# A Mamba round in which DMAs that GpSimd issues add up the softplus, and ScalarE scales a fifth state

## The chip, the cores and the metric

The kernel runs on one core of a Trainium2 chip. The metric is the device time of one execution in microseconds. A core has five engines that are spoken of here: TensorE (PE in the profile, PEld for its weight loads), VectorE (DVE), ScalarE (ACT), GpSimd (POOL) and SyncE (SP), which only issues DMAs. They run side by side and meet only at semaphores. GpSimd can compute and can issue DMAs, one after the other in its own program order.

## The reference

A two-layer model works on `x` of 8 sequences of 512 tokens with 128 features. Layer 0 (attention and a routed feed-forward block) is not touched by the change. Layer 1 is a Mamba block beside a gated feed-forward block:

```python
xv = x @ W_in ; xv = silu(causal_conv(xv, 4 taps) + conv_b)     # 256 channels
ssm = xv @ W_x                                                   # dt_raw (8), B (16), C (16)
delta = softplus(dt_raw @ W_dt + b_dt)
dA  = exp(delta[..., None] * A)                                  # 16 states
dBx = delta[..., None] * B[:, :, None, :] * xv[..., None]
h[l] = dA[l] * h[l-1] + dBx[l]                                   # along the tokens
y = sum over states n of h[..., n] * C[..., n] ; y = y + xv * D
s = y @ W_out
g = silu((silu(x @ wg.T) * (x @ wu.T)) @ wd.T)
out = x_before_norm + s * g
```

## The kernel before, in words

Layer 1 works in rounds, one for each sequence b of 0 to 7, with one round of preparation ahead of them (b = -1) and one of finishing behind them (b = 8). Channels lie on the 128 partitions in KH = 2 halves, the L = 512 tokens along the free dimension. The 16 states are taken in NP = 8 pairs; each engine's part of a round is a loop over the pair q = 0 to 7, and what it does at each q is written out by hand. Order on an engine is program order; nothing is rescheduled. Semaphores (`S[name]`, waited for with `at(round, name, count)`) tie the engines together.

In a round with scans:

- ScalarE (`decays`) writes exp(delta * A) of a pair and half into a PSUM ring `dA` that holds 2 such pieces (RA = 2).
- GpSimd (the `tensor_tensor` in the loop of its `round_`) multiplies the broadcast rows of B (`B_pair(q)`, loaded by SP's DMAs from `bt_dram`) with `du` = delta * xv into the ring `dbx` of 4 pieces (R = 4). In the trace `dbx` is called `nfT_all`, the B rows are `attn_all` (q = 0 to 3) and `nf_all` (q = 4 to 7).
- VectorE (`scans`) runs the recurrence over a piece of 2 states x 512 tokens into a ring called `xnT_all` in the trace.
- TensorE (`project(n)`) multiplies state n of both halves with W_out into one of the two PSUM banks `Gb[n % 2]`. It must find the bank drained of state n - 2.
- The projected state is multiplied with its column of C and added up. For the states in `ON_ACT` ScalarE scales (`scale_state`, into `ts`) and GpSimd adds (`sum_scaled`, into `accP`); for the other twelve VectorE does both in one instruction (`add_state`, into `acc`). `output` on GpSimd then joins the two sums, multiplies with the gate G1 and adds `x_all`.

In the same loops sequence b + 1 is prepared: TensorE makes the convolution of b + 2 (`x_in`), `ssm`, `skip`, `C_rows`, `dt` and the feed-forward products (`ffn_up`, `ffn_down`); VectorE runs `conv_gate` (xv), `ffn_hidden` (fa, hff) and `gate`; ScalarE runs the transcendental functions. TensorE's order is fixed: `ffn_down` stands at q = 5, and starts when VectorE has written the third `hff`; behind it come projections 10 and 11, `x_in(b + 2, 0)`, projections 12 and 13, `x_in(b + 2, 1)`, projections 14 and 15, and then the next round's `ssm` (which needs VectorE's xv), `skip`, projections 0 and 1, `C_rows` and `dt`.

The softplus of sequence b + 1 is computed as relu(z) + ln(1 + e) + (e + (1 - (1 + e))) with e = exp(-|z|); the last bracket is what the rounding of 1 + e lost. ScalarE writes `ab` (e), `rl` (relu), `lg` (the logarithm) and `e1` (1 minus the rounded 1 + e); then GpSimd adds `lg + rl` at its q = 5 (`softplus_high`), `ab + e1` at q = 6 (`softplus_low`) and the two sums into `delta` at q = 7 (`deltas`). Behind the last pair it makes `du` (`drives`). `delta` and `du` are double-buffered by the parity p. Each of the three sums and `du` is one `tensor_tensor` of 128 x 1024 fp32. In the round of preparation the four stand right behind each other.

The outer loop (`rounds`) writes out rounds -1 and 0, loops twice over a body of two rounds (1 and 2, then 3 and 4), and writes out rounds 5 to 8. Rounds -1 to 5 have an `x_in` of a later sequence (`ahead`); round 6 prepares round 7 but has no `x_in`; rounds 7 and 8 prepare nothing.

Of the kernel before, what the change touches and what calls it, by code (L numbers as in the profile page):

```python
# [5 lines left out]
def attention_moe_mamba_ffn(nc, t, out):  # L6
# [15 lines left out]
    P = 128  # L22
# [20 lines left out]
    with ctx:  # L43
# [3 lines left out]
        def sem(name):  # L47
            return ctx.enter_context(nc.semaphore(name))
# [1062 lines left out]
        with ExitStack() as ph:  # L1111
# [4 lines left out]
            RA = 2  # L1116
            ON_ACT = (5, 7, 9, 15)
            ON_DVE = tuple(n for n in range(NS) if n not in ON_ACT)

# [3 lines left out]
            def B_pair(q):  # L1123
# [17 lines left out]
            rl = sb6("rl", [P, KH, L])  # L1141
            lg = sb6("lg", [P, KH, L])
            e1 = sb6("e1", [P, KH, L])
# [9 lines left out]
            s_bld = [sem(f"p6_B_loaded_{q}") for q in range(NP)]  # L1153
            s_o = sem("p6_out_stored")
            names = {"xv_ps": KH, "yh": KH, "tc": KH, "xv": KH, "ff_ps": KF, "tf": KF, "fa": KF, "hf": KF,
                     "ssm_ps": 1, "ssm": 1, "C_ps": 1, "C": 1, "dn_ps": 1, "tg": 1, "G1": 1, "dt_ps": KH, "rl": KH,
                     "ey": 1, "lg": 1, "e1": 1, "corr": 1, "sp": 1, "delta": 1, "du": 1, "acc_ps": 1, "acc0": 1, "t": 1,
                     "ts": len(ON_ACT), "accP": len(ON_ACT),
# [60 lines left out]
            def _(pool):  # L1219
# [5 lines left out]
                def round_(b, p, scan, prep, ahead, end):  # L1225
# [12 lines left out]
                    def output():  # L1238
# [13 lines left out]
                            .then_inc(S["ow"], 1)  # L1252

                    def softplus_high():

                        w("lg", 1)
                        w("rl", KH)
                        w("delta", 0)
                        alone(pool)
                        nc.gpsimd.tensor_tensor(lg[:, :, :], lg[:, :, :], rl[:, :, :], ALU.add).then_inc(S["sp"], 1)  # L1260

                    def softplus_low():
                        w("e1", 1)
                        nc.gpsimd.tensor_tensor(e1[:, :, :], ab[:, :, :], e1[:, :, :], ALU.add)\
                            .then_inc(S["corr"], 1)

                    def deltas():
                        w("sp", 1)
                        w("corr", 1)
                        pool.wait_ge(S["dA"], at(b, "dA", 0))  # L1270
                        pool.wait_ge(S["du"], at(b, "du", 0))
                        nc.gpsimd.tensor_tensor(delta[:, 1 - p, :, :], e1[:, :, :], lg[:, :, :], ALU.add)\
                            .then_inc(S["delta"], 1)

                    def drives():

                        w("delta", 1)
                        w("xv", KH)
                        pool.wait_ge(S["dbx"], at(b, "dbx", 0))
                        nc.gpsimd.tensor_tensor(du[:, 1 - p, :, :], delta[:, 1 - p, :, :], xv[:, :, :], ALU.mult)\  # L1280
                            .then_inc(S["du"], 1)

                    if scan:
                        pool.wait_ge(S["du"], at(b, "du", 1))
                        for q in range(NP):
                            if q == 1 and end:
                                sum_scaled(b - 1, 2)
                            if q == 3 and end:
                                sum_scaled(b - 1, 3)
                                output()  # L1290
# [17 lines left out]
                    elif prep:  # L1308
                        softplus_high()
                        softplus_low()  # L1310
                        deltas()
                        drives()
                    elif end:
                        sum_scaled(b - 1, 2)
                        sum_scaled(b - 1, 3)
                        output()

# [106 lines left out]
            def _(act):  # L1424
                act.wait_ge(s_set, 1)

                def decays(b, p, q):

                    if q == 0:
                        act.wait_ge(S["delta"], at(b, "delta", 1))  # L1430
                    for h in range(KH):
# [28 lines left out]
                def round_(b, p, scan, prep, ahead, end):  # L1460
# [24 lines left out]
                    def abs_relu(h):  # L1485
                        w("dt_ps", h + 1)
                        w("corr", 0)
                        w("lg", 0)
                        w("delta", 0)
                        nc.scalar.activation(ab[:, h, :], bank[bM[h]], ACT.Abs, bias=b_dt[:, h:h + 1])  # L1490
                        nc.scalar.activation(rl[:, h, :], bank[bM[h]], ACT.Relu, bias=b_dt[:, h:h + 1])\
                            .then_inc(S["rl"], 1)
# [5 lines left out]
                    def ln_one_plus():  # L1498
                        w("ey", 1)
                        w("delta", 0)  # L1500
                        nc.scalar.activation(lg[:, :, :], ab[:, :, :], ACT.Ln, bias=1.0).then_inc(S["lg"], 1)  # L1501

                    def one_plus():

                        w("ey", 1)
                        w("delta", 0)
                        nc.scalar.activation(e1[:, :, :], ab[:, :, :], ACT.Identity, bias=1.0).then_inc(S["t"], 1)
# [18 lines left out]
                    for q in range(NP):  # L1526
                        if scan and q + 1 < NP:
                            decays(b, p, q + 1)
                        if q == 0 and end:
                            scale_state(b - 1, 1 - p, 3)  # L1530
                        if scan and 3 <= q < 6:
                            scale_state(b, p, q - 3)
# [157 lines left out]
```

## Time and profile before

| what | value |
|---|---|
| time, median of 3 runs (lowest, highest) | 908.47 us (906.34, 909.36) |
| the profiled execution, its own time | 903.81 us |
| its span from first to last instruction | 901.5 us |
| mean granted TensorE clock | 0.922 of full speed |
| busy in the span: PE, DVE, ACT, POOL | 689.7, 702.3, 471.3, 521.4 us |
| layer 1's first scan, start | 454.3 us |
| layer 1's scans, count and mean | 128 of 2.27 us |

The profile is of one execution; its own time is 2.3 us above its span and 4.7 us under the median of the runs. Busy time of TensorE is modelled (its matmuls are pipelined). The rows of a timeline give start, duration, engine, line, operation, output and inputs, count, and in brackets how long the engine had been idle and what released it. Durations of neighbours on an engine overlap a little at their ends, so that where a sum over a stretch is wanted, the distance of two starts is the better number.

### The profile page before, as it was taken

The numbers are of one execution on the slowest core, as the hardware profiler recorded it, in microseconds if no ns is written. First come the engines' busy times: TensorE is split into PE (matmuls) and PEld (weight loads), VectorE is DVE, ScalarE is ACT, GpSimd is POOL, SyncE is SP. The second block draws the span as 40 slices with busy tenths as digits, with TensorE's granted clock in tenths as the row PEclk, the third lists the DMA queues.
The fourth block names the chain that finished last, engine by engine and source line by source line (L and its number), as shares of the span: only waits on it lengthen the run. The fifth ranks groups of instructions, "written<-read, shape, count | busy, mean of one in ns | idle before, by whom it ended". The sixth has DMA issues, their size and how long they took to land. (4 is left out here: it accounts for less than half of the span.)

```text
span 901.5 us, 14653 instructions
## 1 busy us (share of the span) xinstructions
PE 689.7 (77%) x3968; PEld 507.1 (56%) x3969; DVE 702.3 (78%) x1262; ACT 471.3 (52%) x874; POOL 521.4 (58%) x318
## 2 busy tenths in 40 slices
PE   1884999998777772107677988978889798997764
PEld 0771566556344441103346777766777676786763
DVE  5975687877355554881269999998999999999995
ACT  0431666665122221332568586785867869587451
POOL 0213671000000005730478999999899999999993
PEclk9966999999799996556999999999999999999899
DMA  8400110000211111100521142230322204131000
GB/s 233 165 0 15 33 35 12 0 0 0 74 47 50 52 47 35 44 20 1 187 95 54 42 131 71 46 133 25 130 70 65 111 26 150 49 107 71 25 12 12
DMA packets 40046, 55.79 MB, mean 62 GB/s; under 512 B 6584, under 2 KB 29632, under 8 KB 40000
## 3 DMA queue, kind: packets, MB, share of 16 engines
q1 hardware_dynamic: 36224, 50.48, 16.8%
q0 software_dynamic: 2048, 4.20, 1.6%
q10 hardware_dynamic: 1728, 0.57, 0.3%
q8 instruction: 19, 0.31, 0.1%
q14 instruction: 27, 0.22, 0.1%
HBM read 45.54 MB, written 9.70 MB: 61 GB/s over the span
## 5 line engine op out<-in xcount | busy, mean ns | idle before, releaser
L1585 DVE TENSOR_TENSOR_SCAN xnT_all<-psum,nfT_all 128x1024 f32<-128x1024 f32 x128 | 285.6, 2273 | 7.6 <-ACT psum L1435 4.7
L1323 PEld LDWEIGHTS psum<-W_out,xnT_all 128*128 128x128 f32 x2048 | 241.0, 195 | 37.1 <-issue 35.2
L1323 PE MATMUL psum<-W_out,xnT_all 128*128 128x128 f32 x2048 | 243.9, 278 | 16.4 <-DVE acc L1601 16.4
L1435 ACT ACTIVATE psum<-delta,A 128x511 f32<-128x511 f32 x256 | 163.2, 678 | 41.9 <-DVE xnT_all L1585 41.1
L1303 POOL TENSOR_TENSOR nfT_all<-nf_all,du 128x1024 f32<-128x1024 f32 x64 | 149.9, 2367 | 5.1 <-DVE xnT_all L1585 5.1
L1303 POOL TENSOR_TENSOR nfT_all<-attn_all,du 128x1024 f32<-128x1024 f32 x64 | 149.3, 2361 | 1.4 <-POOL du L1280 0.9
L960 POOL COPY pos_w<-pos 128x4 uint32 x8 | 1.6, 198 | 202.7 <-issue 202.5
L1601 DVE SCALAR_TENSOR_TENSOR acc<-psum,Cc,acc 128x128 f32<-128x128 f32 x352 | 96.7, 342 | 7.8 <-PE psum L1323 7.8
L1323 PE MATMUL psum<-vo_all,wgu 128*128 128x512 f32 (+1 forms) x96 | 46.7, 608 | 31.2 <-DVE hff L1621 29.6
L1323 PE MATMUL psum<-vo_all,W_taps 128*128 (+4 forms) x128 | 60.1, 617 | 1.7 <-DVE psum L1568 1.7
L809 PE MATMUL psum<-gu,xT 128*128 x80 | 46.6, 668 | 15.6 <-DVE hm L892 13.5
L864 ACT ACTIVATE xT<-psum 128x128 f32<-128x128 f32 x40 | 11.1, 278 | 80.4 <-PE psum L797 80.4
L981 PE MATMUL psum<-const,xn 128*128 128x128 f32 x32 | 8.3, 434 | 52.7 <-issue 31.5
L1260 POOL TENSOR_TENSOR lg<-lg,rl 128x1024 f32<-128x1024 f32 x8 | 18.8, 2347 | 49.8 <-ACT lg L1501 49.8
L536 PEld LDWEIGHTS psum<-vo_all,PT 128*128 128x128 f32 x256 | 31.8, 195 | 24.1 <-ACT PT L614 16.3
L1323 PEld LDWEIGHTS psum<-vo_all,wgu 128*128 128x128 f32 x96 | 16.3, 189 | 47.6 <-issue 29.4
L964 POOL DMA_INDIRECT moe_w<-ys_dram,pos_w x32 | 33.7, 1053 | 13.9 <-issue 8.9
L1456 ACT ACTIVATE ts<-psum,Cc 128x128 f32<-128x128 f32 x128 | 35.8, 357 | 10.1 <-PE psum L1323 10.1
L486 POOL DMA_INDIRECT xs_dram<-xs_w,pos_w x32 | 32.4, 1012 | 14.7 <-issue 9.9
L1323 PEld LDWEIGHTS psum<-vo_all,W_taps 128*128 128x128 f32 x128 | 24.3, 199 | 27.7 <-issue 25.6
L905 DVE COPY yt<-psum 128x128 f32<-128x128 f32 x40 | 11.7, 292 | 35.5 <-PE psum L826 35.5
L536 PE MATMUL psum<-vo_all,PT 128*128 (+1 forms) x256 | 38.0, 293 | 1.7 <-ACT PT L614 1.4
(202 smaller groups left out, 1261.4 us busy)
## 6 DMA issues: line engine op xcount, KB each, us to landing
attn_all<-bt_dram SPq DMA_DIRECT2D x32, 512.0 KB, 5.4
nf_all<-bt_dram SPq DMA_DIRECT2D x32, 512.0 KB, 3.6
xs_dram<-zeros SPq DMA_DIRECT2D x4, 640.0 KB, 7.3
xs_t<-xs_dram SPq DMA_DIRECT2D x40, 64.0 KB, 1.8
ys_dram<-yt SPq DMA_DIRECT2D x40, 64.0 KB, 1.6
x_all<-in_x_dram SPq DMA_DIRECT2D x8, 256.0 KB, 6.7
out_dram<-ow SPq DMA_DIRECT2D x8, 256.0 KB, 2.3
gu<-in_gate_dram SPq DMA_DIRECT2D x1, 1024.0 KB, 5.9
```

What stands on the lines that cost most here:

```text
L486: pool.indirect_dma_start(xs_dram, bass.IndirectOffsetOnAxis(ap=pos_w[:, i, j:j + 1], axis=0), xs_w[:, i, j, :], None).then_inc(s_sc[i], 16)
L536: ins = nc.tensor.matmul(bank[4][:, j * P:(j + 1) * P], PT[:, j % 2, c, :], vo_all[:, ds(b * TPB + c, 1), :], start=(c == 0), stop=(c == T ...
L809: nc.tensor.matmul(bank[2 + u % 2], xT[:, u % 2, :], gu_flat[:, ds(e * (2 * I), 2 * I)], start=True, stop=True).then_inc(S["gu_ps"], 1)
L905: nc.vector.tensor_copy(yt[:, u % UN, :], bank[6 + u % 2][:, 0:D]).then_inc(S["y"], 1)
L964: pool.indirect_dma_start(moe_w[:, i, j, :], None, ys_dram, bass.IndirectOffsetOnAxis(ap=pos_w[:, i, j:j + 1], axis=0)).then_inc(s_moe[i], 16)
L1260: nc.gpsimd.tensor_tensor(lg[:, :, :], lg[:, :, :], rl[:, :, :], ALU.add).then_inc(S["sp"], 1)
L1303: nc.gpsimd.tensor_tensor(dbx[:, i % R, :, :], B_pair(q), du[:, p, h:h + 1, :].to_broadcast([P, 2, L]), ALU.mult)\
L1323: return nc.tensor.matmul(o, l, r, start=start, stop=stop)
L1435: ins = nc.scalar.activation(dA[:, i % RA, k, 1:L], delta[:, p, h, 1:L], ACT.Exp, scale=A[:, h, 2 * q + k:2 * q + k + 1])
L1456: ins = nc.scalar.activation(ts[:, i, j, :], bank[Gb[n % 2]][:, j * P:(j + 1) * P], ACT.Copy, scale=Cc[:, p, j, n:n + 1])
L1585: nc.vector.tensor_tensor_scan(hring[:, i % R, :, :].rearrange("p n l -> p (n l)"), dA[:, i % RA, :, :].rearrange("p n l -> p (n l)"), dbx ...
L1601: nc.vector.scalar_tensor_tensor(acc[:, p, j, :], bank[Gb[m % 2]][:, j * P:(j + 1) * P], Cc[:, p, j, m:m + 1], acc[:, p, j, :] if i else s ...
```

## The change

The three sums leave GpSimd's arithmetic. `add_to` issues a DMA on GpSimd's queue that reads `part`, adds it to `total` and writes `total`, and raises a new semaphore `s_sp` by 16 when it has landed. Three such DMAs make a round's 48. ScalarE's logarithm is written straight into `delta[:, 1 - p]` (the buffer `lg` is gone), the first DMA adds `rl` to it, the second adds `ab` to `e1`, and the third adds `e1` to `delta`. The third is issued when the first two have landed (`s_sp` at 32 of the round), `drives` waits until all three have (48), and so does ScalarE before it reads `delta` in `decays` and before it writes `ab` and `rl` again. State 11 moves from VectorE's `add_state` to ScalarE's `scale_state`, in a slot at q = 6, and `sum_scaled` gets a fourth call in a round.

```diff
-            ON_ACT = (5, 7, 9, 15)
+            ON_ACT = (5, 7, 9, 11, 15)
...
-            lg = sb6("lg", [P, KH, L])
...
+            s_sp = sem("p6_softplus_summed")
...
+                    def add_to(total, part):
+                        pool.dma_start(total, part, accum_op=ALU.add).then_inc(s_sp, 16)
+
                     def softplus_high():
-
                         w("lg", 1)
                         w("rl", KH)
-                        w("delta", 0)
                         alone(pool)
-                        nc.gpsimd.tensor_tensor(lg[:, :, :], lg[:, :, :], rl[:, :, :], ALU.add).then_inc(S["sp"], 1)
+                        add_to(delta[:, 1 - p, :, :], rl[:, :, :])
 
                     def softplus_low():
                         w("e1", 1)
-                        nc.gpsimd.tensor_tensor(e1[:, :, :], ab[:, :, :], e1[:, :, :], ALU.add)\
-                            .then_inc(S["corr"], 1)
+                        alone(pool)
+                        add_to(e1[:, :, :], ab[:, :, :])
 
                     def deltas():
-                        w("sp", 1)
-                        w("corr", 1)
-                        pool.wait_ge(S["dA"], at(b, "dA", 0))
-                        pool.wait_ge(S["du"], at(b, "du", 0))
-                        nc.gpsimd.tensor_tensor(delta[:, 1 - p, :, :], e1[:, :, :], lg[:, :, :], ALU.add)\
-                            .then_inc(S["delta"], 1)
+                        pool.wait_ge(s_sp, (b + 1) * 48 + 32)
+                        alone(pool)
+                        add_to(delta[:, 1 - p, :, :], e1[:, :, :])
 
                     def drives():
 
-                        w("delta", 1)
+                        pool.wait_ge(s_sp, (b + 2) * 48)
                         w("xv", KH)
...
-                            if q == 1 and end:
-                                sum_scaled(b - 1, 2)
+                            if q in (1, 2) and end:
+                                sum_scaled(b - 1, q + 1)
                             if q == 3 and end:
-                                sum_scaled(b - 1, 3)
+                                sum_scaled(b - 1, 4)
                                 output()
...
                     if q == 0:
-                        act.wait_ge(S["delta"], at(b, "delta", 1))
+                        act.wait_ge(s_sp, (b + 1) * 48)
+                        alone(act)
...
-                        nc.scalar.activation(lg[:, :, :], ab[:, :, :], ACT.Ln, bias=1.0).then_inc(S["lg"], 1)
+                        nc.scalar.activation(delta[:, 1 - p, :, :], ab[:, :, :], ACT.Ln, bias=1.0).then_inc(S["lg"], 1)
...
                         if q == 0 and end:
-                            scale_state(b - 1, 1 - p, 3)
-                        if scan and 3 <= q < 6:
+                            scale_state(b - 1, 1 - p, 4)
+                        if scan and 3 <= q < 7:
                             scale_state(b, p, q - 3)
```

On GpSimd, from the round of preparation through round 0, the program stood before like this (`nfT_all` is the ring `dbx`):

```order
L1260 TENSOR_TENSOR lg<-lg,rl 128x1024
L1264 TENSOR_TENSOR e<-ab,e 128x1024
L1272 TENSOR_TENSOR delta<-e,lg 128x1024
L1280 TENSOR_TENSOR du<-delta,xv 128x1024
L1303 TENSOR_TENSOR nfT_all<-attn_all,du 128x1024 x8
L1303 TENSOR_TENSOR nfT_all<-nf_all,du 128x1024 x2
L1260 TENSOR_TENSOR lg<-lg,rl 128x1024
L1303 TENSOR_TENSOR nfT_all<-nf_all,du 128x1024 x2
L1264 TENSOR_TENSOR e<-ab,e 128x1024
L1303 TENSOR_TENSOR nfT_all<-nf_all,du 128x1024 x2
L1272 TENSOR_TENSOR delta<-e,lg 128x1024
L1235 TENSOR_TENSOR accP<-ts 128x512
```

and it stands now like this:

```order
L1255 DMA delta<-rl 128x1024
L1255 DMA e<-ab 128x1024
L1255 DMA delta<-e 128x1024
L1278 TENSOR_TENSOR du<-delta,xv 128x1024
L1301 TENSOR_TENSOR nfT_all<-attn_all,du 128x1024 x8
L1301 TENSOR_TENSOR nfT_all<-nf_all,du 128x1024 x2
L1255 DMA delta<-rl 128x1024
L1301 TENSOR_TENSOR nfT_all<-nf_all,du 128x1024 x2
L1255 DMA e<-ab 128x1024
L1301 TENSOR_TENSOR nfT_all<-nf_all,du 128x1024 x2
L1255 DMA delta<-e 128x1024
L1235 TENSOR_TENSOR accP<-ts 128x512
```

Each of the three sums has turned into a DMA issue at the same place; nothing lies between the three at the top, and two instructions of the ring lie between each two of those in the round.

On VectorE, in round 0, between the scans of pairs 6 and 7, the four instructions of state 11 are gone (`xnT_all` is what the scans write):

```order
 L1585 SCALAR_TENSOR_TENSOR xnT_all<-psum,nfT_all 128x1024 x2
-L1601 SCALAR_TENSOR_TENSOR acc<-psum,Cc,acc 128x128 x8
+L1601 SCALAR_TENSOR_TENSOR acc<-psum,Cc,acc 128x128 x4
 L1627 SCALAR_TENSOR_TENSOR G<-tg,psum 128x512
 L1585 SCALAR_TENSOR_TENSOR xnT_all<-psum,nfT_all 128x1024 x2
```

They moved to ScalarE, at its q = 6, behind the decays of pair 7 and ahead of the convolution's tanh:

```order
 L1524 ACTIVATE tg<-psum 128x512
 L1435 ACTIVATE psum<-delta,A 128x511 x4
+L1456 ACTIVATE ts<-psum,Cc 128x128 x4
 L1443 ACTIVATE tconv<-psum,convb 128x512
 L1446 ACTIVATE psum<-psum,convb 128x512
```

TensorE's order is the same as before.

## Rows read from the trace of the kernel before

**Rows 1.** Busy time by stretch: stretch, length, then busy time (instructions) of PE, PEld, DVE, ACT, POOL

```profile
700.00:760.00 60.00, 52.87 (x356) 42.44 (x355) 58.55 (x82) 44.81 (x77) 59.41 (x29) 1.00 0.25 90
```

**Rows 2.** Timeline of VectorE, from one third hff to the next

```profile
716.93 0.69 DVE L1621 SCALAR_TENSOR_TENSOR hff<-fa,psum 128x512 f32<-128x512 f32 x1
...
724.31 1.13 DVE L1601 SCALAR_TENSOR_TENSOR acc<-psum,Cc,acc 128x128 f32<-128x128 f32 x4 [0.27 <-PE psum L1323]
...
745.62 1.13 DVE L1601 SCALAR_TENSOR_TENSOR acc<-psum,Cc,acc 128x128 f32<-128x128 f32 x4 [0.66 <-PE psum L1323]
...
771.59 0.69 DVE L1621 SCALAR_TENSOR_TENSOR hff<-fa,psum 128x512 f32<-128x512 f32 x1
```

**Rows 3.** Timeline of TensorE behind that hff, and its busy time there

```profile
717.67 2.94 PE L1323 MATMUL psum<-wd,hff 128*128 128x128 f32 x24 [1.16 <-DVE hff L1621]
...
727.45 3.73 PE L1323 MATMUL psum<-W_out,xnT_all 128*128 128x128 f32 x32
...
738.11 1.91 PE L1323 MATMUL psum<-xv,W_x 128*40 128x512 f32 x4
...
717.60:756.70 39.10, 38.92 (x264) 1.00 0.25 86
```

**Rows 4.** Timeline of ScalarE in the same stretch

```profile
727.73 0.69 ACT L1443 ACTIVATE tconv<-psum,convb 128x512 f32<-128x512 f32 x1 [3.37 <-PE psum L1323]
...
729.04 2.71 ACT L1435 ACTIVATE psum<-delta,A 128x511 f32<-128x511 f32 x4
```

**Rows 5.** Timeline of GpSimd, a steady round and the next du

```profile
708.97 2.35 POOL L1264 TENSOR_TENSOR e<-ab,e 128x1024 f32<-128x1024 f32 x1 [0.22 <-ACT e L1511]
...
715.91 2.38 POOL L1272 TENSOR_TENSOR delta<-e,lg 128x1024 f32<-128x1024 f32 x1
718.23 1.28 POOL L1235 TENSOR_TENSOR accP<-ts 128x512 f32<-128x512 f32 x1
...
724.10 2.36 POOL L1280 TENSOR_TENSOR du<-delta,xv 128x1024 f32<-128x1024 f32 x1
...
778.84 2.36 POOL L1280 TENSOR_TENSOR du<-delta,xv 128x1024 f32<-128x1024 f32 x1
```

**Rows 6.** B loads of 512 KB (ns, landing); GpSimd's indirect issues; busy times, last columns DMA share, GB/s

```profile
L1212 SPq DMA_DIRECT2D nf_all<-bt_dram x32: 327/333/649, 430.0 to 833.6; - x32
...
DMA to landing us min/median/max: 3.3/3.6/9.9
...
L964 POOL DMA_INDIRECT moe_w<-ys_dram,pos_w x32: 943/956/1543, 344.4 to 391.7; - x32
...
  issue: 8.9, 26
...
435.00:440.00 5.00, 1.96 (x4) 0.68 (x4) 1.72 (x3) 4.94 (x6) 2.07 (x1) 1.00 1.02 395
```

**Rows 7.** Timelines of GpSimd, ScalarE and VectorE from preparation to the first scan

```profile
441.74 2.34 POOL L1264 TENSOR_TENSOR e<-ab,e 128x1024 f32<-128x1024 f32 x1 [1.47 <-ACT e L1511]
...
449.08 18.52 POOL L1303 TENSOR_TENSOR nfT_all<-attn_all,du 128x1024 f32<-128x1024 f32 x8
...
453.02 2.51 ACT L1435 ACTIVATE psum<-delta,A 128x511 f32<-128x511 f32 x4
...
454.34 4.47 DVE L1585 TENSOR_TENSOR_SCAN xnT_all<-psum,nfT_all 128x1024 f32<-128x1024 f32 x2 [4.74 <-ACT psum L1435]
```

**Rows 8.** VectorE behind the loop's jump back, TensorE's waits, VectorE in rounds 6 and 7

```profile
622.88 4.47 DVE L1585 TENSOR_TENSOR_SCAN xnT_all<-psum,nfT_all 128x1024 f32<-128x1024 f32 x2 [2.64 <-POOL nfT_all L1303]
...
PE psum L1323 <- DVE xv L1611: 2.6, 1, 2.6
...
833.56 1.12 DVE L1601 SCALAR_TENSOR_TENSOR acc<-psum,Cc,acc 128x128 f32<-128x128 f32 x4 [0.18 <-PE psum L1323]
834.60 0.68 DVE L1627 SCALAR_TENSOR_TENSOR G<-tg,psum 128x512 f32<-128x512 f32 x1
...
880.75 2.14 DVE L1601 SCALAR_TENSOR_TENSOR acc<-psum,Cc,acc 128x128 f32<-128x128 f32 x8
```

More of the change, by code:

```diff
@@ L1154, in attention_moe_mamba_ffn @@
             s_o = sem("p6_out_stored")
+            s_sp = sem("p6_softplus_summed")
             names = {"xv_ps": KH, "yh": KH, "tc": KH, "xv": KH, "ff_ps": KF, "tf": KF, "fa": KF, "hf": KF,
                      "ssm_ps": 1, "ssm": 1, "C_ps": 1, "C": 1, "dn_ps": 1, "tg": 1, "G1": 1, "dt_ps": KH, "rl": KH,
-                     "ey": 1, "lg": 1, "e1": 1, "corr": 1, "sp": 1, "delta": 1, "du": 1, "acc_ps": 1, "acc0": 1, "t": 1,
+                     "ey": 1, "lg": 1, "e1": 1, "du": 1, "acc_ps": 1, "acc0": 1, "t": 1,
                      "ts": len(ON_ACT), "accP": len(ON_ACT),
@@ L1315, in round_ @@
                         sum_scaled(b - 1, 3)
+                        sum_scaled(b - 1, 4)
                         output()
@@ L1486, in abs_relu @@
                         w("dt_ps", h + 1)
-                        w("corr", 0)
-                        w("lg", 0)
-                        w("delta", 0)
+                        if scan:
+                            act.wait_ge(s_sp, (b + 1) * 48)
+                            alone(act)
                         nc.scalar.activation(ab[:, h, :], bank[bM[h]], ACT.Abs, bias=b_dt[:, h:h + 1])
@@ L1499, in ln_one_plus @@
                         w("ey", 1)
-                        w("delta", 0)
-                        nc.scalar.activation(lg[:, :, :], ab[:, :, :], ACT.Ln, bias=1.0).then_inc(S["lg"], 1)
+                        act.wait_ge(S["du"], at(b, "du", 0))
+                        act.wait_ge(S["dA"], at(b, "dA", 0))
+                        nc.scalar.activation(delta[:, 1 - p, :, :], ab[:, :, :], ACT.Ln, bias=1.0).then_inc(S["lg"], 1)
                     def one_plus():
                         w("ey", 1)
-                        w("delta", 0)
                         nc.scalar.activation(e1[:, :, :], ab[:, :, :], ACT.Identity, bias=1.0).then_inc(S["t"], 1)
```

## The prediction, made before the changed kernel ran

> **What bounds the kernel now.** I read the busy time by stretch first. In a steady stretch of 60 us GpSimd is busy for 59.4 us and VectorE for 58.6, TensorE for 52.9 and ScalarE for 44.8 [rows 1]. By that view GpSimd and VectorE share the bound, and the change takes work from both. The second view, the timelines, says something else, and the prediction hangs on it.
>
> A round is 54.7 us long: GpSimd's du starts at 724.10 and 778.84 [rows 5]. I split the round at two events on VectorE [rows 2]. The third hff is written from 716.93. From there VectorE does not set the pace: it waits for TensorE 0.27 us before state 11 and 0.66 us before state 1 of the next sequence, whose sum starts at 745.62. TensorE starts its down projection at 717.67, released by that hff, and from 717.60 to 756.70 it is busy for 38.92 of 39.10 us at full clock, with no wait recorded; the next round's first product with W_x, in the middle, starts at 738.11 [rows 3]. So those 28.7 us (716.93 to 745.62) are TensorE's: one chain of matmuls from the third hff to the projections of states 0 and 1. The other 26.0 us (745.62 to 771.59, the next third hff) are VectorE's, which has no wait there that I found. 28.7 + 26.0 = 54.7: the period closes. GpSimd has its own 54.7 us, but waits 0.22 us for ScalarE's e1 in it [rows 5], so it is the third, almost equal loop, some 0.2 to 0.4 us from the bound.
>
> **State 11 off VectorE.** Its four instructions stand at q = 6, between the third hff and state 1, thus in TensorE's part. Their step is 1.04 us (833.56 to 834.60) [rows 8], and the wait of 0.2 to 0.3 us before them goes too. In rounds 0 to 5 VectorE just waits those 1.3 us longer at states 0 and 1: nothing gained. On ScalarE the four take the place of idle time: before the tanh at 727.73 it waits 3.37 us for TensorE, and four of its instructions with 511 columns take 2.71 us [rows 4], so that these four with 128 take less. TensorE needs state 11's bank drained for projection 13; ScalarE is free from 727.73 - 3.37 = 724.36, so the bank is drained by 727.1 at the latest, and TensorE comes to projection 13 near 729.3, half way through the 3.73 us behind 727.45 [rows 3]. Without that cover it would cost the difference each round.
>
> Three places are left where VectorE's 1.2 us count. Round 6 has no x_in, so TensorE's chain is 7 us shorter there and VectorE is the bound: state 11 and its wait of 0.18 go, 1.2 us [rows 8]. In round 7 VectorE runs without a gap: half of the 2.14 us at 880.75, 1.0 us [rows 8]. And at the loop's jump back VectorE stands still for 2.64 us before 622.88, upon which TensorE waits 2.6 us for xv [rows 8]; there VectorE's lead of 1.2 us shortens the wait. Sum of the gains: 3.4 us.
>
> **Three sums off GpSimd, one accP addition on.** A round on GpSimd loses 3 x 2.36 and the wait of 0.22 and gains 1.28: 54.7 - 7.1 - 0.2 + 1.3 = 48.7 us, plus three issues [rows 5]. No accumulating DMA is in the trace. The nearest row for an issue is an indirect DMA on the same queue: 0.96 us, and 8.9 us of idle time before 26 of them, 0.34 each, so 1.3 us [rows 6]. GpSimd then needs 52.6 us of 54.7 and has 2.1 us for waits.
>
> **How long such a DMA takes (T, from issue to landing).** A plain load of the same 512 KB lands after 3.6 us, 3.3 at least and 9.9 at most [rows 6]. An issue on GpSimd takes 0.6 us more than one on SP (0.96 against 0.33 [rows 6]), and I add that. The add needs a second read; at the 395 GB/s of a stretch in which the DMA engines are full, 512 KB take 1.3 us [rows 6]. T = 3.6 + 0.6 + 1.3 = 5.5 us. For the range the bounds are 3.3 and 9.9.
>
> The Trainium skill prices this from its own fit: its page "DMA: Bandwidth & Descriptors", section "Anatomy of one DMA — SWDGE (gpsimd) path", gives a fixed 2.0 us and the bytes at 436 GB/s, which is 3.2 us here, and "Collectives: The Full Stack" (section "The bandwidth ceiling: the fold count and why AG ≠ RS ≠ AR") says that an add reads two sources at half the rate; an estimate by both is 4.4 us, by which the sum below would be 2.2 us lower.
>
> **Steady rounds.** The second DMA is issued when e1 is there; two ring pieces of 2.32 us each (18.52 for eight [rows 7]) follow. GpSimd comes to the third issue 1.3 + 4.6 = 6.0 us later, and from there to du after 1.3 + 1.3 + 4.6 = 7.2 us. Waits are T - 6.0 and T - 7.2 where positive. They eat the 2.1 us at T = 7.65: below it rounds keep their 54.7 us, above it each of the seven rounds 0 to 6 grows by 2 (T - 7.65). ScalarE, which now waits for the third DMA before its decays of the next round's first pair (729.04 [rows 4]), is reached well after the landing: 708.97 + 6.0 + 5.5 = 720.5. Behind that wait stand the tanh of the second half and then all decays, so it would matter from T of about 10.
>
> **Preparation.** Here nothing covers them. The second sum starts at 441.74, when ScalarE's e1 is there, and the ring is begun at 449.08 [rows 7]. Now: 441.74 + T (second lands) + T (third lands) + 2.36 for du [rows 5] + 2.32 for the first ring piece + 0.3 for the handoffs (my estimate), against the first scan's start at 454.34, which ScalarE's decays of 453.02 set [rows 7]: a loss of 2T - 7.6, zero below 3.8, and 3.4 us at 5.5. TensorE waits for VectorE's xv behind it, so the loss stays.
>
> **The sum.** 3.4 - 3.4 = 0 on the profiled 903.8 us. The median of the runs is 4.7 us above the profiled time; I predict 908.5 us.
>
> **Rivals.**
> 1. T is the price that I misjudge. At its low bound the preparation costs nothing: -3.4 us, 905.1. Between 6.85 and 7.65 the loss is 2.7 to 4.3 us, to 912.8. For the low end speaks that this traffic never leaves the core's memory; for the high end that the B loads, issued as each pair's pieces are done, share the engines.
> 2. GpSimd becomes the bound (the slower side). Place: the third issue and du. It decides from T = 7.65. At T = 9: 10.4 in preparation, 7 x 2.7 = 18.9 in the rounds, less 3.4: +26 us, 934. At 9.9: +40. Against it stand the 2.15 us between my T and that point; for it, that the second and third DMA of a round each meet a B load, whose 1.3 us of transfer would bring them to 6.8, and that an add may cost the DMA engines more than its second read.
> 3. VectorE's freed time counts in every round (my reading of TensorE as the bound is wrong; its busy time is modelled): six more rounds at 1.2: -7.2, 901.3. For it speaks VectorE's 58.6 of 60 us; against it, that the period closes without it.
> 4. VectorE holds up the issues. A scan lasts 2.27 us on average; if each issue had to wait for one, it would take 3.6 us, and GpSimd 48.7 + 10.8 = 59.5: +4.8 x 7 = +33 us, 942. Against it: the indirect issues took 0.94 to 1.54 us [rows 6]. "SBUF — State Buffer" of the Trainium skill, section "SBUF: two separate sides", has such a lock on GpSimd's descriptors, by VectorE's two-port modes; every VectorE instruction of these rounds has an operand in PSUM, so by that rule it should not occur, and no run so far shows it.
>
> **Chances.** My forecast, T from 4.15 to 6.85 with rounds unchanged: 0.42; the sum is then within 2.7 us, which is the 0.3% that a measurement of this kernel can tell from no change. T shorter: 0.10. VectorE's time counts: 0.10. T from 6.85 to 7.65: 0.10. GpSimd bound: 0.23. Issues held up: 0.05. So faster 0.20, same 0.42, slower 0.38. The range leaves out rival 3 and the part of rivals 2 and 4 beyond T = 8.5 (9.4 + 11.9 - 3.4 = +18): 904 to 926. The forecast's own range is 905.8 to 911.2.
>
> **What the profile would show.** Landing of the new DMAs near 5.5 us. A first scan near 457.7 instead of 454.34. Steady du starts 54.7 us apart, VectorE's waits for TensorE before states 0 and 1 longer by 1.3 us in sum, GpSimd idle for about 2 us a round. It is wrong if GpSimd waits before du or at the third issue in steady rounds, if TensorE shows waits between the third hff and state 1, or if an issue takes over 2 us.

## The result and the profile after

| | before | after |
|---|---|---|
| median of 15 runs each, same chip (lowest to highest) | 906.81 us (902.23 to 910.57) | 901.07 us (898.62 to 904.48) |
| ratio, 95% interval | | 0.9942 [0.9922, 0.9962] |
| profiled execution, its own time / span | 903.8 / 901.5 us | 904.48 / 902.0 us |

The change is worth 5.3 us (3.5 to 7.1). It is faster, 3 us under the stated range. The profiled execution of after is the slowest of its 15 runs, and that of before was near its fastest. Layer 0, which the change does not touch, differs by up to 7.5 us between the fourteen profiles of this document (ScalarE's first tanh of layer 1's convolution, near the start of the round of preparation, begins anywhere from 413.2 to 420.6 us; 416.4 to 420.0 in the three profiles of after). So every comparison below is of differences inside one trace, from that tanh on. Two executions among the experiments, of 1225 and 1431 us, were slow ones and count in no ratio.

**Steady rounds, VectorE.** The timeline of after, round behind the loop's jump back first, then a steady hff, then the last one:

```profile
609.93 0.69 DVE L1621 SCALAR_TENSOR_TENSOR hff<-fa,psum 128x512 f32<-128x512 f32 x1
...
617.56 4.47 DVE L1585 TENSOR_TENSOR_SCAN xnT_all<-psum,nfT_all 128x1024 f32<-128x1024 f32 x2
622.52 1.13 DVE L1601 SCALAR_TENSOR_TENSOR acc<-psum,Cc,acc 128x128 f32<-128x128 f32 x4 [0.50 <-PE psum L1322]
624.31 1.13 DVE L1601 SCALAR_TENSOR_TENSOR acc<-psum,Cc,acc 128x128 f32<-128x128 f32 x4 [0.66 <-PE psum L1322]
625.35 4.46 DVE L1585 TENSOR_TENSOR_SCAN xnT_all<-psum,nfT_all 128x1024 f32<-128x1024 f32 x2
629.73 1.26 DVE L1611 SCALAR_TENSOR_TENSOR xv<-tconv,psum 128x512 f32<-128x512 f32 x2
...
774.12 0.69 DVE L1621 SCALAR_TENSOR_TENSOR hff<-fa,psum 128x512 f32<-128x512 f32 x1
...
828.78 0.69 DVE L1621 SCALAR_TENSOR_TENSOR hff<-fa,psum 128x512 f32<-128x512 f32 x1
```

Two things are to be seen. The steady step from third hff to third hff is 54.66 us (774.12 to 828.78), where [rows 2] had 54.66: the four instructions of state 11 are gone from VectorE and the round is as long as it was. And behind 617.56, where [rows 8] have the 2.64 us stall of the jump back, the scan at 625.35 follows the sum before it without a gap. The waits of VectorE between 470 and 860 us (engine, name, line, for what: us in total, times, longest):

```profile
DVE acc L1601 <- PE psum L1322: 17.8, 26, 3.3
```

In that stretch it is now the one kind of wait that VectorE has, and it is for TensorE. (The longest, 3.3 us at 472.64, belongs to the first round; before has one of 3.0 us at 467.41, ahead of the stretch.)

**GpSimd.** Its timeline, preparation first, then from the third DMA of round 4 to the du of round 5, and the second DMA of round 5:

```profile
440.27 0.99 POOL L1255 DMA_DIRECT2D delta<-rl  x1 [45.61 <-ACT delta L1502]
444.13 0.89 POOL L1255 DMA_DIRECT2D e<-ab  x1 [2.87 <-ACT e L1511]
449.84 0.85 POOL L1255 DMA_DIRECT2D delta<-e  x1 [4.81 <-DMA e<-ab]
454.33 2.34 POOL L1278 TENSOR_TENSOR du<-delta,xv 128x1024 f32<-128x1024 f32 x1 [3.64 <-DMA delta<-e]
...
717.90 1.21 POOL L1255 DMA_DIRECT2D delta<-e  x1
718.48 1.93 POOL L1235 TENSOR_TENSOR accP<-ts 128x512 f32<-128x512 f32 x1
719.71 5.34 POOL L1301 TENSOR_TENSOR nfT_all<-nf_all,du 128x1024 f32<-128x1024 f32 x2
725.60 2.37 POOL L1278 TENSOR_TENSOR du<-delta,xv 128x1024 f32<-128x1024 f32 x1 [0.56 <-DMA delta<-e]
...
767.53 0.88 POOL L1255 DMA_DIRECT2D e<-ab  x1 [2.80 <-ACT e L1511]
```

The wait for ScalarE's e1 has grown from 0.22 us [rows 5] to 2.80: that is the slack. The wait of 0.56 us before du is for the third DMA. Landing times, in the page's list of DMA issues (KB each, median us from issue to landing):

```profile
delta<-rl POOLq DMA_DIRECT2D x8, 512.0 KB, 6.3
e<-ab POOLq DMA_DIRECT2D x8, 512.0 KB, 4.6
delta<-e POOLq DMA_DIRECT2D x8, 512.0 KB, 7.5
```

**The first scan** comes at 459.19, waiting for GpSimd's first ring piece, and TensorE's down projection ahead of it ran slowly (VectorE's and TensorE's timeline):

```profile
447.17 4.29 PE L1322 MATMUL psum<-wd,hff 128*128 128x128 f32 x24 [2.13 <-DVE hff L1621]
...
459.19 4.59 DVE L1585 TENSOR_TENSOR_SCAN xnT_all<-psum,nfT_all 128x1024 f32<-128x1024 f32 x2 [6.38 <-POOL nfT_all L1301]
```

### The profile page after: what moved, and what is told of

It is laid out like the page before. It is cut to its first block and busy times, and to the rows that moved or that the text cites. A ratio compares the mean times of both kernels' runs of the same rounds, so it can differ in the third digit from the quotient of the medians.

```text
span 902.0 us, 14650 instructions
## 1 busy us (share of the span) xinstructions
PE 698.6 (77%) x3968; PEld 513.6 (57%) x3969; DVE 694.5 (77%) x1230; ACT 479.2 (53%) x906; POOL 497.9 (55%) x326
## 5 line engine op out<-in xcount | busy, mean ns | idle before, releaser
L1322 PEld LDWEIGHTS psum<-W_out,xnT_all 128*128 128x128 f32 x2048 | 244.3, 197 | 38.3 <-issue 35.9
L1322 PE MATMUL psum<-W_out,xnT_all 128*128 128x128 f32 x2048 | 246.6, 280 | 15.7 <-DVE acc L1601 15.7
L1301 POOL TENSOR_TENSOR nfT_all<-nf_all,du 128x1024 f32<-128x1024 f32 x64 | 158.3, 2632 | 2.6 <-DVE xnT_all L1585 2.6
L1601 DVE SCALAR_TENSOR_TENSOR acc<-psum,Cc,acc 128x128 f32<-128x128 f32 x320 | 88.5, 342 | 13.0 <-PE psum L1322 13.0
L1322 PE MATMUL psum<-vo_all,wgu 128*128 128x512 f32 (+1 forms) x96 | 49.2, 637 | 26.5 <-DVE hff L1621 24.9
L1456 ACT ACTIVATE ts<-psum,Cc 128x128 f32<-128x128 f32 x160 | 44.7, 357 | 8.0 <-PE psum L1322 8.0
L486 POOL DMA_INDIRECT xs_dram<-xs_w,pos_w x32 | 32.4, 1014 | 14.5 <-issue 9.7
L981 PEld LDWEIGHTS psum<-const,xn 128*128 128x128 f32 x32 | 5.7, 216 | 54.9 <-issue 53.9
```

Source lines behind the costliest of these rows:

```text
L486: pool.indirect_dma_start(xs_dram, bass.IndirectOffsetOnAxis(ap=pos_w[:, i, j:j + 1], axis=0), xs_w[:, i, j, :], None).then_inc(s_sc[i], 16)
L981: ins = nc.tensor.transpose(bank[i][:, j * P:(j + 1) * P], xn1[:, i, j, :], ident)
L1301: nc.gpsimd.tensor_tensor(dbx[:, i % R, :, :], B_pair(q), du[:, p, h:h + 1, :].to_broadcast([P, 2, L]), ALU.mult)\
L1322: return nc.tensor.matmul(o, l, r, start=start, stop=stop)
L1456: ins = nc.scalar.activation(ts[:, i, j, :], bank[Gb[n % 2]][:, j * P:(j + 1) * P], ACT.Copy, scale=Cc[:, p, j, n:n + 1])
L1601: nc.vector.scalar_tensor_tensor(acc[:, p, j, :], bank[Gb[m % 2]][:, j * P:(j + 1) * P], Cc[:, p, j, m:m + 1], acc[:, p, j, :] if i else s ...
```

## The experiments

Twelve runs follow, in three groups: before once more, after twice more, and eight new kernels, one of them twice. The groups are e1, e2, e3 and e6; e4, e5, e7 and e8; e9 to e12. Each ran on one chip together with the kernel before. Ratios are to the kernel before of the same group, with 95% intervals. "Step 3" is the step from third hff to third hff that holds the loop's jump back; the other five steps are 54.65 to 54.77 us in every kernel but one (the sums on GpSimd, below). The tail is from the last third hff to the end, the preparation from ScalarE's first tanh of the convolution to VectorE's first scan, and the down projection is TensorE's 24 matmuls in it.

| kernel | time, us | ratio | step 3 | tail | preparation | down projection |
|---|---|---|---|---|---|---|
| before, first profile | 906.81 | 1 | 57.46 | 75.24 | 36.17 | 2.94 |
| e1 before again | 906.86 | 1.0000 [0.9976, 1.0024] | 58.82 | 74.91 | 37.85 | 4.58 |
| e2 DMAs only | 906.45 | 0.9999 [0.9975, 1.0023] | 57.19 | 75.68 | 38.99 | 4.58 |
| e3 sums on GpSimd | 910.47 | 1.0048 [1.0026, 1.0070] | 55.04 | 77.93 | 37.84 | 4.51 |
| e4 before, loop written out | 901.45 | 0.9956 [0.9940, 0.9971] | 54.66 | 75.72 | 37.46 | 4.57 |
| e5 after, loop written out | 901.98 | 0.9959 [0.9940, 0.9978] | 54.66 | 72.85 | 38.94 | 4.39 |
| e6 preparation's sums on GpSimd | 901.71 | 0.9952 [0.9930, 0.9974] | 54.75 | 73.20 | 36.17 | 2.94 |
| e7 after, body padded | 903.48 | 0.9981 [0.9964, 0.9998] | 57.21 | 72.73 | 38.08 | 4.55 |
| e8 after again | 900.53 | 0.9951 [0.9934, 0.9968] | 54.76 | 73.17 | 38.80 | 4.41 |
| e9 as e6, again | 898.82 | 0.9922 [0.9896, 0.9948] | 54.75 | 73.20 | 38.25 | 4.50 |
| e10 one sum back | 900.36 | 0.9946 [0.9927, 0.9965] | 54.75 | 73.25 | 37.85 | 4.58 |
| e11 two sums back | 900.51 | 0.9948 [0.9931, 0.9966] | 54.75 | 74.84 | 37.81 | 4.40 |
| e12 after, third time | 899.28 | 0.9937 [0.9916, 0.9958] | 54.76 | 73.19 | 38.56 | 4.66 |
| after, first profile | 901.07 | 0.9942 [0.9922, 0.9962] | 54.76 | 73.22 | 39.16 | 4.29 |

**e1, the kernel before once more**, to see which parts of its profile vary.

> The kernel before, unchanged, against itself: how far two equal kernels differ in this measurement, and a second profile of it. Chance (the rival that the 5.7 us of the change are an accident of the runs): a ratio away from 1 by 0.3% or more. My theory: 1.000 within 0.2%. In the trace I look for the 2.6 us that VectorE stood still behind the jump back of the loop: if it belongs to every execution it is there again; if it comes and goes, it may be missing or stand elsewhere.

The step with the jump back is 58.82 us, longer still than in the first profile, and the profile names the stall otherwise. VectorE's timeline of e1:

```profile
623.01 2.13 DVE L1601 SCALAR_TENSOR_TENSOR acc<-psum,Cc,acc 128x128 f32<-128x128 f32 x8
627.54 4.47 DVE L1585 TENSOR_TENSOR_SCAN xnT_all<-psum,nfT_all 128x1024 f32<-128x1024 f32 x2 [2.39 <-issue]
...
640.58 1.13 DVE L1601 SCALAR_TENSOR_TENSOR acc<-psum,Cc,skip_sb 128x128 f32<-128x128 f32 x4 [1.98 <-PE psum L1323]
```

"issue" is time in which the engine waited for nothing that the profile shows. Here the mark is right: what the scan at 627.54 needs was there before VectorE stood still at 625.14. GpSimd had written the two pieces of that pair by 624.1 us, and ScalarE its decays by 624.4 (begun at 621.72, 2.71 us):

```profile
619.41 4.68 POOL L1303 TENSOR_TENSOR nfT_all<-attn_all,du 128x1024 f32<-128x1024 f32 x2 [0.27 <-POOL du L1280]
```

So the "POOL nfT_all" of [rows 8] was only the last event before the scan. What does fall into the idle time is a fetch of instructions. In the DMA view of e1, cut to 625.2 to 627.5 us, the only packet on any queue is this one (queue, packets, MB, share):

```profile
q14 instruction: 1, 0.01, 1.3%
```

The second wait, 1.98 us at 640.58 where the first profile of before has 0.36, is TensorE at a lower clock right behind the stall (stretch, length, PE busy, clock granted as a share of full speed, DMA share, GB/s):

```profile
628.00:632.00 4.00, 2.86 (x26) 1.00 0.00 0
632.00:636.00 4.00, 2.76 (x4) 0.64 0.00 0
```

TensorE had waited 2.38 us for xv before 633.24. 0.64 is a mean over the stretch of the two levels, 1.2 and 2.4 GHz. In the first profile a wait of 2.6 us [rows 8] was not followed by a lower clock, and step 3 was 1.4 us shorter.

**e2, the DMAs without state 11's move.** The three sums are DMAs, VectorE keeps state 11.

```diff
-ON_ACT = (5, 7, 9, 11, 15)
+ON_ACT = (5, 7, 9, 15)
```

(with sum_scaled and scale_state in the places that they have before.)

> The three sums as DMAs, state 11 left with VectorE. Theory A (rounds are held by TensorE's chain plus VectorE's part; the change gains in rounds 6 and 7 by state 11 and otherwise only where a stall of one execution is taken up by slack): nothing of the 2.0 us of state 11, the whole loss of 2.5 to 2.9 us in preparation, so within 0.3% of before, 905 to 910 us. Theory B (GpSimd was the bound in most executions, and its relief is the gain): 900 to 903 us with state 11 where it was.

Nothing is gained: 0.9999. Between 500 and 860 us GpSimd is not busy for 32.5 us (360 less 327.5), against 7.5 and 9.5 in the two profiles of before, and waits the difference out. The stall stays, at the same place:

```profile
627.99 4.47 DVE L1584 TENSOR_TENSOR_SCAN xnT_all<-psum,nfT_all 128x1024 f32<-128x1024 f32 x2 [2.39 <-issue]
```

**e3, state 11's move without the DMAs.**

```diff
-pool.dma_start(total, part, accum_op=ALU.add).then_inc(s_sp, 16)
+nc.gpsimd.tensor_tensor(total, total, part, ALU.add).then_inc(s_sp, 16)
```

> All of the change but the DMAs: the logarithm goes into delta, state 11 is ScalarE's, and the three sums are additions on GpSimd again. GpSimd then has 54.7 + 1.3 - 0.2 = 55.8 us a round. Both theories: GpSimd becomes the bound in rounds 1 to 6, +1.1 us each, less 2.0 us for rounds 6 and 7: +4 to +6 us on before, and steady du starts 55.8 us apart. If VectorE's time counted in every round (my rival 3) it could not show here. It tells how much of a GpSimd that is over the bound comes through.

This is where GpSimd becomes the bound: its round holds one accP addition more and no sum less. The steps are 54.75, 54.76, 55.04, 55.70, 55.47 and 56.37 us, 3.5 us more than six steady ones; the 55.8 us expected are reached only from the fourth on. The tail is longer too. Between 700 and 870 us VectorE waits 3.5 us for TensorE, where e8 has 4.5, and 4.8 us are marked "issue". These are waits for GpSimd all the same. The longest ends 0.1 us after GpSimd has written the first of two ring pieces of 2.33 us each (the other four end likewise):

```profile
863.30 4.66 POOL L1301 TENSOR_TENSOR nfT_all<-attn_all,du 128x1024 f32<-128x1024 f32 x2
865.74 4.60 DVE L1585 TENSOR_TENSOR_SCAN xnT_all<-psum,nfT_all 128x1024 f32<-128x1024 f32 x2 [2.73 <-issue]
```

So "issue" alone tells nothing; one has to look when the inputs were ready. The stall at the jump back is gone, and that by state 11's move alone. VectorE's timeline of e3 there:

```profile
619.88 1.13 DVE L1601 SCALAR_TENSOR_TENSOR acc<-psum,Cc,acc 128x128 f32<-128x128 f32 x4 [0.51 <-PE psum L1322]
621.67 1.13 DVE L1601 SCALAR_TENSOR_TENSOR acc<-psum,Cc,acc 128x128 f32<-128x128 f32 x4 [0.66 <-PE psum L1322]
622.71 4.46 DVE L1585 TENSOR_TENSOR_SCAN xnT_all<-psum,nfT_all 128x1024 f32<-128x1024 f32 x2
```

**e4 and e5, no jump at all**: before and after, with the loop over the middle rounds written out.

```diff
-with eng.Fori(0, (NB - 4) // 2) as r:
+for r in range((NB - 4) // 2):
```

> The kernel before with the loop over rounds 1 to 4 written out, so that no engine jumps back there. Theory A (VectorE's stall of 2.4 to 2.6 us belongs to the jump back of a loop body that does not stay in VectorE's instruction store): all six steps 54.7 us, 2.7 to 4.1 us under the kernel before, ratio 0.996. Rival (the stall comes from GpSimd's ring or from DMAs at that point of round 3): the long step of 57.2 to 58.8 us stays, ratio 1.000.

> The changed kernel with the same loop written out. Theory A: it has no stall at the jump, so nothing is gained: ratio to before 0.994, the same as the changed kernel within 0.2%. If the jump costs anything else on any engine, it is faster than the changed kernel.

e4 is before without any part of the change, and it is 0.44% faster, nearly as much as the whole change in the same group (0.49%, e8). Its timeline of VectorE has no stall:

```profile
618.35 2.13 DVE L1601 SCALAR_TENSOR_TENSOR acc<-psum,Cc,acc 128x128 f32<-128x128 f32 x8
620.40 4.46 DVE L1585 TENSOR_TENSOR_SCAN xnT_all<-psum,nfT_all 128x1024 f32<-128x1024 f32 x2
```

e5 gains nothing over after (0.9959 against 0.9951 of e8 in the same group): after had no stall left to remove.

**e7, the body made long again.** After, with 24 one-column instructions in VectorE's loop body, 12 a round, which read and write nothing that is used, where VectorE waits for TensorE anyhow.

```diff
+if q == 6 and not isinstance(b, int):
+    for i in range(12):
+        nc.vector.memset(dry[:, i:i + 1], 0.0)
```

> The changed kernel with 24 instructions of one column (12 a round) put back on VectorE in the loop body alone, where VectorE waits 1.2 us for TensorE; they add some 0.7 us of work there and no dependency. Theory A: the body is longer than before the change, the stall of 2.4 us at the jump back is there again, one step of 56.0 to 57.5 us, and the time is 1.5 to 3 us over the changed kernel, ratio to before 0.996 to 0.998. If length has nothing to do with it and it is state 11's own waits that stalled, all steps stay 54.8 and the ratio 0.994.

They take 0.21 us a dozen, and the stall is back, 2.42 us. VectorE's timeline of e7:

```profile
609.84 0.21 DVE L1651 MEMSET dry<- 128x1 f32 x12
...
616.56 1.12 DVE L1603 SCALAR_TENSOR_TENSOR acc<-psum,Cc,acc 128x128 f32<-128x128 f32 x4 [0.61 <-PE psum L1324]
620.10 4.47 DVE L1587 TENSOR_TENSOR_SCAN xnT_all<-psum,nfT_all 128x1024 f32<-128x1024 f32 x2 [2.42 <-issue]
```

The time rises by 2.95 us over e8 in the same group (903.48 against 900.53; the intervals of the two ratios just touch), step 3 by 2.45, and the other steps stay. The profile page's rows of instruction traffic (queue, packets, MB, share) move with it. Of e7:

```profile
q14 instruction: 27, 0.22, 0.1%
```

and of after:

```profile
q14 instruction: 22, 0.18, 0.1%
```

Before, e1, e2 and e7 have 27 packets and the stall; after, e6, e8, e9, e10, e11 and e12 have 22, e3 23, and no stall at the jump; e4 and e5, which are longer programs without a jump there, have 24. When the packets come says more than how many they are. Between 616 and 700 us, from just ahead of the jump into the second pass through the loop, before has

```profile
q14 instruction: 5, 0.04, 0.2%
```

and after and e8 have none. In the four profiles with the stall (before, e1, e2, e7) one packet starts 0.3 to 0.5 us after VectorE's last sum ahead of the jump has ended (at 620.77, 625.42, 625.87 and 617.99 us), and VectorE's scan starts 2.1 us behind it in all four. The loop's body for VectorE, counted in the built program with its waits and register arithmetic, is 336 instructions in before, e1 and e2, 320 in after and e3, 344 in e7.

**e6 and e9, the preparation's three sums back on GpSimd**, the same kernel in two groups.

```diff
+if scan:
     pool.dma_start(total, part, accum_op=ALU.add).then_inc(s_sp, 16)
+else:
+    nc.gpsimd.tensor_tensor(total, total, part, ALU.add).then_inc(s_pp, 16)
```

> The changed kernel with the three sums of the round of preparation, where nothing covers a DMA, as additions on GpSimd; the rounds with scans keep the DMAs. Theory A: the first scan comes 16.4 us after the logarithm (before 16.4, after 18.9), 2.5 us earlier than after, and the time is 2.5 to 2.9 us under the changed kernel: ratio to before 0.991, 898 us. If the loss in preparation is made good later anyway, the time is that of the changed kernel, 901 us.

> The changed kernel with the preparation's three sums as additions on GpSimd, once more. Theory A: from the first tanh to the first scan 36.2 to 37.9 us against 38.8 to 39.2, so 1 to 3 us under the changed kernel beside it. Rival, after the first run of it (901.7 against 901.1): the additions give nothing in most executions, because TensorE's down projection at its lower clock then sets the first scan; the median stays within 0.5 us of the changed kernel.

Both forecasts missed; the rivals named beside them, that the time is that of the changed kernel, came true. e6 is 901.71 us beside 906.63 of before, no better than after had been; e9 is 898.82 beside e12's 899.28, 0.5 us in place of 1 to 3, which the intervals do not separate. e6's preparation is 36.17 us, e9's 38.25. The difference is TensorE's down projection, 2.94 us in e6 and in the first profile of before, 4.3 to 4.7 in the twelve other profiles. TensorE's granted clock in e9 (columns as above):

```profile
436.00:442.00 6.00, 3.78 (x7) 0.78 0.35 139
442.00:447.00 5.00, 2.87 (x10) 0.50 0.00 0
447.00:452.00 5.00, 5.00 (x24) 0.87 0.00 0
```

From 442 to 447 us TensorE is busy for 2.87 of 5 us, having waited 2.1 to 2.2 us for each hff, and gets 0.50 of its clock, which is the lower of its two levels; in the first profile of before it had 1.00 with the same pattern of work.

**e8 and e12, after again**, as neighbours of the other runs of their groups.

> The changed kernel once more, for a second profile and a second comparison on this chip. Theory A: ratio near 0.994; third hff to third hff 54.7 to 54.8 us in all six steps, with no longer step behind the loop's jump back; last third hff to the end 73.2 us. If the missing stall was an accident of one execution, one step is 57 us or more.

> The changed kernel a third time, so that the three kernels beside it can be set against it on the same chip. 901 us, ratio to before 0.994 to 0.995; from the convolution's first tanh to the first scan 38.8 to 39.2 us.

All three measurements of after lie within 0.0014 of each other; steps, tail and preparation repeat within 0.6 us.

**e10 and e11, one and two sums back on GpSimd in every round**, to measure how much of what the DMAs free is needed.

```diff
-alone(pool)
-add_to(e1[:, :, :], ab[:, :, :])
+nc.gpsimd.tensor_tensor(e1[:, :, :], ab[:, :, :], e1[:, :, :], ALU.add).then_inc(S["corr"], 1)
```

(e11: the first sum in the same manner, so that only the third is a DMA.)

> The second sum (ab + e1) as an addition on GpSimd again, in all rounds; the first and third stay DMAs. In the preparation the chain is one addition and one DMA, 2.35 + 4.5 us in place of 5.7 + 4.5: the first scan 1 to 3 us earlier. In the rounds GpSimd gets 2.35 for 0.9 us, 1.45 more, of 2.5 to 3.3 us that it idles now: steps of the third hff stay 54.7 to 54.8. Theory A: as e9, 1 to 3 us under the changed kernel. If GpSimd's idle time is no real slack, the steps grow by up to 1.4.

> The first two sums as additions on GpSimd, only the third as a DMA. GpSimd gets 2.9 us more than in the changed kernel, about all of its idle time: steps 54.7 to 55.2 us. Theory A: this is the edge, at most 3 us over e10. If the bound of the rounds were GpSimd already in the changed kernel, the steps would be 57.

Steps are 54.75 us in both, though the time between 500 and 860 us in which GpSimd is not busy falls from 24.0 us (after) to 15.0 and 7.2. GpSimd's waits between 500 and 840 us, e8 first (all three DMAs):

```profile
POOL e L1255 <- ACT e L1511: 14.1, 6, 2.7
POOL du L1278 <- DMA delta<-e: 3.4, 7, 0.6
```

then e11:

```profile
POOL du L1280 <- DMA delta<-e: 4.0, 7, 0.7
```

With two sums back the wait for ScalarE is used up, and what is left is the wait for the third DMA. e10 was expected 1 to 3 us faster than after and is not (900.36 beside 899.28). Its preparation is 37.85 us beside e12's 38.56. One of the three DMAs is enough to carry state 11's move through rounds 0 to 6. In round 7 it is not quite enough: e11's tail is 1.65 us longer than e12's, 1.15 us of that an idle time before the scan at 855.30 that is marked "issue" and ends, as in e3, 0.1 us after GpSimd's ring piece begun at 852.86. At the same place after, e8 and e12 have 0.40, 0.23 and 0.41 us. e11 is at 900.51 beside 899.28, which the intervals do not separate.

## Why the prediction was wrong

**What held.** The split of the round. TensorE's chain and VectorE's part close the period, and taking VectorE's state 11 out of TensorE's part left every steady step at 54.7 us, in nine profiles. VectorE waits instead, though earlier than forecast: 0.50 and 0.66 us before 622.52 and 624.31, which are states 12 and 13 and had no wait before. At states 0 and 1, where the wait was expected to grow, it is 1.08 us in a steady round of after and was 1.05 in before. Over 470 to 860 us its waits for TensorE are 14.5 us in e8, where before had 8.4 in the same stretch. Rival 3 (VectorE's time counts in every round, 901.3) came closest to the measured time and is refuted by the steps: it needed 53.5 us, and they are 54.7. The right number would have come from the wrong mechanism.

GpSimd has the slack that was forecast, 2.1 us a round and a little more: in e8 it waits 14.1 us for e1 in six rounds and 3.4 us for the third DMA in seven, 2.8 us a round. But T for the third DMA is 7.5 us, not 5.5, and GpSimd waits 0.56 us before du in a steady round, which the forecast had named as a sign of being wrong; its own formula, T - 7.2, gives 0.3 us at the measured T. The rounds did not grow, because the second DMA lands after 4.6 us and is not waited for. With that one free, the same formulas put the point from which rounds grow at 9.3 us for the third (7.2 + 2.1), and not at 7.65 for both. Issues took 0.85 to 1.23 us, so rival 4 did not occur.

Rounds 6 and 7: forecast -2.2 us; the tail is 75.39 us in the mean of before, e1, e2 and e4 and 73.11 in the mean of after, e5, e8 and e12: -2.3.

**The step that failed.** "at the loop's jump back VectorE stands still for 2.64 us before 622.88 ...; there VectorE's lead of 1.2 us shortens the wait." The stall was read as a wait that VectorE could meet earlier or later, and priced as the lead. It isn't a wait for any engine: in e1 all inputs were there when it began. It appears with a loop body of 336 or 344 instructions and not with 320 (e2, e7 against e3, e8), not when the jump is gone (e4), and it does not depend on who makes the sums (e2, e3). There is no lead at that point either: with state 11 gone VectorE waits for TensorE at states 12 and 13, ahead of the jump, and comes to the jump 15.4 us after the third hff in after as in e4. So the stall was not shortened but went entirely: step 3 is 57.82 us in the mean of before, e1 and e2 and 54.76 in after, e8 and e12, -3.1 us (-2.4 to -4.1, the larger when TensorE's clock drops behind it) where the sum had -1.2. It is the fetching of instructions: 27 packets for 22 or 23, 0.04 MB more, wherever the stall is at the jump; one of them inside the stall, and the scan 2.1 us behind that packet's start in four profiles; none on that queue between 616 and 700 us in after and e8, which have no stall.

The Trainium skill has this mechanism: its page "Runtime: NRT & Kernel Launch", section "Instruction fetch mechanics", says that an engine keeps only a small window of its program and that a taken branch to a target outside it has to fetch first. The trace agrees, with 27 packets and 2.39 to 2.64 us against 22 and none. The page gives most engines a window of 512 instructions, refilled in blocks of 256 (16 KiB); here the packets carry 8 KB each (0.22 MB in 27), and a body of 336 instructions stalls where one of 320 does not. With a window that moves by whole blocks, what decides may be where the body lies in the blocks as much as how long it is; no run here changed the one without the other.

**The term that was mis-sized: preparation.** Forecast 2T - 7.6 = +3.4 us at T = 5.5. From the second issue to the third are 5.7 us (444.13 to 449.84), and from there to du 4.5 (449.84 to 454.33): 10.2 for 11. From the second issue to the first scan after needs 15.06 us, where before needed 12.60 from its second sum [rows 7]: +2.5. But that is against the profile of before as it happened to be taken. With the down projection slow, 4.3 to 4.7 us as in twelve of fourteen profiles, ScalarE's decays come later anyway, and part of the DMAs' time is covered by it: the preparation is 37.85 us in the mean of e1, e3, e4 and e9 (no DMA in it) and 38.76 in the mean of after, e2, e5, e7, e8 and e12 (three DMAs), +0.9 us. This is why e6 and e9 found little to win back.

**The sum by what was measured:** -2.3 (tail) - 3.1 (jump back) + 0.9 (preparation) = -4.5 us; the three comparisons say -5.7, -4.7 and -5.8 us by medians (0.9942, 0.9951, 0.9937). The missing 1 us is inside their intervals of +-1.5 to 1.9 us and has no place that I could name. Against the forecast of 0: -1.9 from the jump back, -2.5 from the preparation, -0.1 from the tail. The predicted 908.5 also stood 1.7 us above the 906.81 that before had in the comparison.

**What stays open.** The trace names the packets' queue but not the engine that a packet is for; that those in the stall are VectorE's rests on when they come. The stall begins somewhere between a body of 320 and one of 336 instructions here; no length between was run, and length is not separated from place. Why the clock dropped behind the stall in e1 and not in before or e2, and in the preparation in most executions but not all, is open too. e4 and e5 should differ by the tail less the preparation, some 1.4 us, and were measured 0.5 us the other way round; their intervals overlap, with only six runs of e4, but this is not explained.

## What to carry to other kernels

An idle time at a loop's jump back may belong to no engine: before pricing it as a wait, check in the timelines when the instruction's inputs were ready, and look whether an instruction packet falls into it. The profile's mark is not enough; the same stall was marked with an engine's name in one profile and "issue" in others, and other idle times marked "issue" were waits for GpSimd. Sixteen instructions less in a body of 336, or the loop written out, gave 3 us here, more than the work that they did. Taking work off two busy engines gave nothing in any steady round here, because a third engine's chain closed the period; follow the period from one event to its next occurrence, and count for each engine where in it the work stands. And a cost read from one profile of a short serial stretch needs a second profile: here the stretch moved by 1.7 us with TensorE's clock alone.

## What the hardware showed that I had not expected

- VectorE's stall at the jump back: 2.39, 2.39, 2.42 and 2.64 us in four profiles, and its absence in a body 16 instructions shorter. An instruction packet starts 0.3 to 0.5 us into it, and VectorE goes on 2.1 us after that packet's start.
- Its after-effect: behind a wait of 2.38 us TensorE was granted 0.64 for 4 us in one execution (e1) and VectorE waited 1.98 us for it; in others with the same stall nothing followed.
- An accumulating DMA of 512 KB within the core's memory: 6.3, 4.6 and 7.5 us (medians) from issue to landing for the first, second and third of a round, 5.1 and 4.4 for the second and third of the preparation, where no load of B ran beside them. The issue keeps GpSimd for 0.85 to 1.23 us in the trace, but its next instruction starts 0.58 us after the issue's start (717.90 and 718.48) and is longer by as much (1.93 us in place of 1.28). Two ring pieces beside such a DMA took 5.34 us in place of 4.66.
